# Units of 32 samples throughout a compressed-interaction kernel: triple products as stationary weights in four column groups, 154-column triple-product matmuls, and a GpSimd that only gathers

## The chip, the cores and the metric

The kernel runs on one core of a Trainium2 chip. The metric is device time in microseconds (us). A core has a matrix engine (PE, with its weight loads shown as PEld), a vector engine (DVE), an activation engine (ACT), GpSimd (POOL) and a sync engine that issues DMAs (SP). PE writes to PSUM, here eight banks of 512 fp32 columns by 128 partitions. ACT and DVE copy from PSUM to SBUF. All data is fp32, and in this trace each fp32 matmul leaves two MATMUL records and each pair of them two LDWEIGHTS records; below, a "record" is one of these halves. Transposes leave one.

## What is computed

For 512 samples, 32 embedding rows of 64 numbers are gathered (one from each of 32 tables), and two compressed-interaction layers, each summed over the 64 dimensions, feed a small network of three layers:

```python
# X[b, m, d]: 32 gathered rows of 64 numbers per sample
x1 = einsum('oc,bcd->bod', W0, outer(X, X))   + b0      # 128 outputs
x2 = einsum('oc,bcd->bod', W1, outer(X, x1))  + b1      # 128 outputs
z  = concat([x1.sum(d), x2.sum(d)])                      # (512, 256)
h  = relu([z, dense_ctx] @ W_top1 + b_top1)              # 512
h  = relu(h @ W_top2 + b_top2)                           # 256
y  = h @ W_top3                                          # (512, 1)
```

The kernel doesn't build x1. It uses that x2 summed over d is a sum over triples: T[m, (i, j)] = sum over d of X_m X_i X_j, with a coefficient for each triple and output that is made once from W1 and W0.

## The kernel before

A **unit** is 32 samples, a **chunk** four units; there are 4 chunks, so 16 units, written below as u = 0 to 15 (q = chunk, s = unit in it). All engine programs are written out by hand; the order in each engine's list is the order of execution, and semaphores join them.

**Gathers.** POOL issues 8 indirect DMAs of 128 rows for each unit (L413), into one of four row buffers; it waits only until the buffer's earlier unit has been transposed. At gather 50 (`FOLD_AT`) POOL stops to do two product instructions of unit 3 and six adds of the coefficient fold.

**Per unit.** PE transposes the gathered rows into bank XT (`transpose_rows`, L193, 4 records); this waits for the gathers and until ACT has emptied the bank of the unit before (`xx_ready`, `gram_ready`). ACT copies XT out as `xx` (`act_xx`, L241, two copies) and into the last columns of `prod` (`act_gram`, L250, two copies). DVE multiplies pairs of `xx` into `prod` (`products`, L261 and L265). PE then forms the triple products in four T groups of 8 samples (`t_group`, L212): 32 matmuls each, of 64 rows by 32 weight columns on 77 moving columns, on eight tiles of the array (two row groups, four column groups). Groups 0 and 2 go to one pair of banks, 1 and 3 to the other, so group 2 waits until group 0 has been copied out. ACT copies groups 0 and 2, DVE 1 and 3, each with one instruction of 128 x 616 (`copy_t`, L229 and L226), into `t_sb`.

**Per chunk.** `cin` (L371) multiplies: 77 matmuls with 128 x 128 coefficients as weights and the chunk's 128 samples as moving columns, accumulated in ACC (x2) and ACC + 1 (x1). The chunk before is done in four quarters, one after the T groups of each unit of this chunk. ACT's `copy_z` (L379) adds the bias.

**Phases.** While unit 0 to 3 are worked on, PE also makes the coefficients (L280, L286, 32 pairs of matmuls, copied out by ACT at L292 and DVE at L296). Then these are folded (L306: DVE 18 adds, POOL 6), transposed by PE (L343, 69 matmuls) and copied (L548, L356). From unit 4 on a step is: four T groups, the transposes of unit u + 2, a quarter of `cin`. After unit 15's T groups the last chunk's 77 `cin` matmuls follow, then the network (L474 dense part, L482, L491, L499).

## Time and profile before

| | us |
|---|---|
| median of 3 runs | 257.38 (256.95 to 258.59) |
| the profiled execution's own time | 258.26 |
| its span, first to last instruction | 256.5 |
| mean granted TensorE clock | 0.939 |

| engine | busy us | share of span |
|---|---|---|
| PE | 209.3 | 82% |
| PEld | 173.8 | 68% |
| POOL | 148.8 | 58% |
| DVE | 127.2 | 50% |
| ACT | 84.4 | 33% |

An engine's busy time is the union of its records. A matmul's end is modelled, so for PE the distance between starts of successive records tells more than the length of one. "idle before <-X" names what ended the idle time ahead of an instruction; "issue" means that the profile shows nothing it waited for. The rows themselves stand in a section of their own below.

### The profile page before, as it was taken

What the parts mean: (1) busy time and instruction counts of PE and PEld (TensorE: products, weight loads), DVE (VectorE), ACT (ScalarE), POOL (GpSimd) and SP (SyncE); (2) the same over time, 40 slices, a digit from 0 to 9 for tenths busy, and PEclk for the clock granted to TensorE, in tenths of its full rate; (3) what the DMA queues carried; (4) which work ended last, traced back from release to release, by engine and by line L of the source; (5) the groups of instructions that cost most, each with busy time, mean ns of one, the idle gap of its engine ahead of it and who ended that gap; (6) DMA issues with size and microseconds to landing.
All of it is one profiled execution on the core that took longest, in us unless ns stands there. A gap on an engine that the chain in (4) does not pass through costs nothing.

```text
span 256.5 us, 10809 instructions
## 1 busy us (share of the span) xinstructions
PE 209.3 (82%) x5049; PEld 173.8 (68%) x5049; DVE 127.2 (50%) x194; ACT 84.4 (33%) x159; POOL 148.8 (58%) x142
## 2 busy tenths in 40 slices
PE   7897899499007889799898796979698896999995
PEld 6664667287006769688787584968697796899541
DVE  0559487666920866838649548173918641000000
ACT  2575447264202961413433313142313310100141
POOL 4778788877899778778778778777750000000000
PEclk9999799979856999999999999799889997999999
DMA  6811111112810111111111111111110000000000
GB/s 206 299 26 20 31 28 23 24 33 35 279 22 3 23 26 25 30 23 31 30 24 30 27 24 31 20 32 28 29 26 3 5 3 5 0 3 0 0 0 0
DMA packets 6564, 9.66 MB, mean 38 GB/s; under 512 B 2804, under 2 KB 3256, under 8 KB 6520
## 3 DMA queue, kind: packets, MB, share of 16 engines
q0 software_dynamic: 4096, 4.20, 9.1%
q1 hardware_dynamic: 2136, 4.19, 4.7%
q8 instruction: 39, 0.64, 1.0%
q10 hardware_dynamic: 288, 0.59, 0.7%
q14 instruction: 5, 0.04, 0.0%
HBM read 8.97 MB, written 0.00 MB: 35 GB/s over the span
## 4 chain that ended last, share of the span: by engine, by line
POOL 43%; PE 36%; issue 15%; DMA 3%; ACT 2%; DVE 0%; DVEq 0%; ACTq 0%; POOLq 0%
POOL rows L413 39%; PE psum L371 19%; PE psum L212 7%; PE psum L491 3%; PE psum L482 3%; DMA rows<-table,idx 2%; POOL t_sb L306 2%; POOL prod L261 2%; PE psum L280 1%; PE psum L193 1%; PE psum L286 1%; ACT t_sb L229 1%; DMA t_sb<-ids 1%; PE psum L474 0%; ACT prod L250 0%
## 5 line engine op out<-in xcount | busy, mean ns | idle before, releaser
L413 POOL DMA_INDIRECT rows<-table,idx x128 | 138.8, 1085 | 40.6 <-issue 38.1
L212 PE MATMUL psum<-prod,xx 64*32 64x77 f32 x4096 | 63.7, 243 | 23.7 <-POOL prod L261 13.4
L261 DVE TENSOR_TENSOR prod<-xx 128x1024 f32<-128x1024 f32 x62 | 73.7, 1220 | 6.8 <-ACT xx L241 4.0
L212 PEld LDWEIGHTS psum<-prod,xx 64*32 64x32 f32 x4096 | 51.4, 109 | 35.9 <-issue 16.2
L371 PE MATMUL psum<-t_sb,coef 128*128 128x128 f32 x552 | 67.9, 285 | 2.1 <-issue 2.1
L371 PEld LDWEIGHTS psum<-t_sb,coef 128*128 128x128 f32 x552 | 66.7, 202 | 2.4 <-issue 2.2
L229 ACT ACTIVATE t_sb<-psum 128x616 f32<-128x616 f32 x34 | 23.3, 685 | 79.8 <-PE psum L212 79.8
L226 DVE COPY t_sb<-psum 128x616 f32<-128x616 f32 x30 | 23.9, 798 | 49.8 <-PE psum L212 49.6
L292 ACT ACTIVATE t_sb<-psum 128x276 f32<-128x276 f32 x32 | 20.7, 647 | 18.2 <-PE psum L280 18.0
L241 ACT ACTIVATE xx<-psum 128x512 f32<-128x512 f32 x32 | 17.5, 595 | 24.2 <-PE psum L193 24.2
L280 PE MATMUL psum<-w0p_sb,w_sb 128*128 128x276 f32 x64 | 21.8, 423 | 1.2 <-DVE w0p_sb L592 0.6
L193 PE MATMUL psum<-ident,rows 128*128 128x128 f32 x64 | 10.3, 284 | 13.3 <-DMA rows<-table,idx 9.5
L286 PE MATMUL psum<-w0x_sb,w_sb 128*128 128x256 f32 x64 | 20.5, 402 | 0.7 <-ACT t_sb L292 0.4
L660 DVE COPY prod<-psum 1x128 f32<-1x128 f32 x2 | 0.6, 292 | 41.2 <-PE psum L499 41.2
L296 DVE COPY coef<-psum 128x256 f32<-128x256 f32 x32 | 13.6, 424 | 10.8 <-PE psum L286 10.8
L193 PEld LDWEIGHTS psum<-ident,rows 128*128 128x128 f32 x64 | 6.9, 141 | 16.2 <-DMA rows<-table,idx 11.7
L286 PEld LDWEIGHTS psum<-w0x_sb,w_sb 128*128 128x128 f32 x64 | 10.7, 189 | 7.3 <-ACT t_sb L292 5.1
L280 PEld LDWEIGHTS psum<-w0p_sb,w_sb 128*128 128x128 f32 x64 | 11.4, 196 | 4.3 <-DVE coef L296 1.2
L379 ACT ACTIVATE w_sb<-psum,cin_bias 128x128 f32<-128x128 f32 x8 | 2.9, 368 | 32.3 <-PE psum L371 32.3
L250 ACT ACTIVATE prod<-psum 128x256 f32<-128x256 f32 x32 | 13.1, 408 | 0.0
L343 PE MATMUL psum<-ident,t_sb 128*128 128x128 f32 x69 | 9.2, 289 | 1.5 <-ACT coef L548 1.4
L356 DVE COPY coef<-psum 128x512 f32<-128x512 f32 (+1 forms) x6 | 3.7, 620 | 12.6 <-POOL t_sb L306 11.5
(33 smaller groups left out, 99.9 us busy)
## 6 DMA issues: line engine op xcount, KB each, us to landing
rows<-table,idx POOLq DMA_INDIRECT x128
w_sb<-w1t SPq DMA_DIRECT2D x3, 512.0 KB, 7.0
w_sb<-top SPq DMA_DIRECT2D x2, 512.0 KB, 5.3
t_sb<-w0x ACTq DMA_DIRECT2D x1, 512.0 KB, 4.8
w0x_sb<-w0g SPq DMA_DIRECT2D x1, 512.0 KB, 3.8
w_sb<-w1t SPq DMA_DIRECT2D x1, 384.0 KB, 5.6
t_sb<-w0p SPq DMA_DIRECT2D x1, 276.0 KB, 5.0
w_sb<-w1t SPq DMA_DIRECT2D x1, 128.0 KB, 4.8
```

What stands on the lines that cost most here:

```text
L193: last = pe.matmul(bank(XT, 128 * t, 128), rows[:, c:c + 2 * D], ident[:, :], is_transpose=True, start=True, stop=True)
L212: last = pe.matmul(bank(TG + 2 * (v % 2) + r, n * COLS, COLS, 32 * (2 * e + k), M), xx[s % 2][D * r:D * (r + 1), x:x + M], prod[2 * (s % 2 ...
L226: copy(dst, src).then_inc(t_copied[v % 2], 1)
L229: copy_t(act, lambda o, i: act.activation(o, i, ACT.Copy), q, t_at, s, v)
L241: act.activation(dst, src, ACT.Copy).then_inc(xx_ready, 1)
L261: last = dve.tensor_tensor(at(p, e * COLS, [[2 * COLS, SUB], [HALF, SHIFTS], [1, HALF]]), at(x, x0, [[M, SUB], [0, SHIFTS], [1, HALF]]), a ...
L280: pe.matmul(bank(W_BANKS[2 * x % 3], 0, 4 * VCOLS), w, w0p_sb[:, :], start=True, stop=True)\
L286: pe.matmul(bank(W_BANKS[(2 * x + 1) % 3], 0, HALF * HALF), w, w0x_sb[:, c:c + HALF * HALF], start=True, stop=True).then_inc(u_done, 1)
L292: act.activation(at(t_sb, coef_t_at + x, [[M, 4], [128, VCOLS]]), src, ACT.Copy).then_inc(u_pairs, 1)
L296: dve.tensor_copy(cross[:, x * HALF * HALF:(x + 1) * HALF * HALF], bank(W_BANKS[(2 * x + 1) % 3], 0, HALF * HALF)).then_inc(u_cross, 1)
L371: last = pe.matmul(bank(n, 0, CHUNK), w[:, wc:wc + O], t_sb[:, t_at + tc:t_at + tc + CHUNK], start=first, stop=end)
L413: pool.indirect_dma_start(rows[:, c:c + D], None, table[:, :], bass.IndirectOffsetOnAxis(ap=idx[:, g:g + 1], axis=0))\
```

## The change

Everything is done per unit of 32 samples; chunks are gone.

- **T groups** (`t_group`): the two halves (e) of a sample's pairs stand side by side in `prod` and are now one moving operand of 154 columns. 16 matmuls a group in place of 32. Samples, no longer halves, fill the column groups, so the result lies differently in PSUM.
- **Copies out** (`copy_t`): each group needs four copies of 64 partitions x 308 in place of one of 128 x 616, since partition halves have to change places. ACT does all four of groups 0 and 2 and two of groups 1 and 3; DVE does the other two of groups 1 and 3. For unit 3 ACT does all.
- **`cin_part` and `cin_tile`**: operands swap places. The triple products of 32 samples are the weights (128 rows x 32 columns), the 128 coefficients' outputs move. Matmul i goes to column group i % 4, so that four partial sums stand in four partition groups of one bank. A unit is 77 matmuls in four parts (25, 17, 17, 18), 1,232 in all where `cin` had 308.
- **`copy_acc` and `fold_z`**: DVE copies the four partial sums (128 x 256) to SBUF, and PE multiplies them with four stacked 32 x 32 identities (`fold4`, made by two small DVE adds), which adds them up and turns them round: two matmuls with 128 x 128 weights and 32 moving columns for each unit. ACT's `copy_z` is two copies of 128 x 32 for each unit.
- **Order from unit 4 on**: five `cin` parts a step, two of them between T groups 1 and 2. The transposes of unit u + 2 follow T group 3; for the last four units (`late`) a step transposes unit u + 1 and its `xx`, gram and product work follows in the same step.
- **GpSimd** only gathers. Its two products and six adds go to DVE. The gathers themselves keep their number and size.
- After unit 15's T groups only unit 15's own 77 `cin` matmuls are left before the network.

```diff
-        def t_group(pe, q, s, v):
+        def t_group(pe, u, v):
...
-            wait(pe, t_copied[v % 2], 2 * u + v // 2)
-            for n in range(GROUP // 2):
-                j = (v % 2) * GROUP // 2 + n
-                for k in range(2):
-                    for e in range(2):
+            for n in range(2):
+                wait(pe, t_copied[n], copied(n, 4 * u + v - 1))
+            for n in range(2):
+                for p in range(2):
+                    j = 4 * (v % 2) + 2 * p + n
+                    x, y = (SUB // 2 * g + j) * 2 * M + HALF, 4 * j * COLS
+                    for k in range(2):
                         for r in range(2):
...
+                            last = pe.matmul(bank(TG + 2 * (v % 2) + r, 2 * n * COLS, 2 * COLS, 32 * (2 * p + k), M),
...
+        def copy_t(eng, copy, n, u, v):
+
+            for p in range(2):
+                if copier(4 * u + v, p) != n:
+                    continue
...
+                for e in range(2):
+                    src = at(psum, (TG + 2 * (v % 2)) * BANK + e * COLS, [[1, COLS], [BANK, 2], [2 * COLS, 2]], D * p, D)
+                    dst = at(t_sb, t_at(u) + v * GROUP + 4 * p, [[UNIT, COLS], [2, 2], [1, 2]], D * e, D)
+                    last = copy(dst, src)
+                last.then_inc(t_copied[n], 1)
...
+        def cin_tile(pe, u, j, n, col, w, start, stop):
+            c = t_at(u) + col * UNIT
+            return pe.matmul(at(psum, acc(u) + n * O, [[1, O]], UNIT * j, UNIT), t_sb[:, c:c + UNIT], w,
+                             start=start, stop=stop, tile_position=(0, UNIT * j))
...
+        def copy_acc(eng, copy, u):
+
+            eng.wait_ge(cin_done, u + 1)
+            wait(eng, z_done, u - 1)
+            copy(acc_sb[u % 2][:, :], at(psum, acc(u), [[1, 2 * O]])).then_inc(acc_copied, 1)
+
+        def fold_z(pe, u):
+
+            pe.wait_ge(acc_copied, u + 1)
...
+            for n in range(2):
+                last = pe.matmul(bank(Z, n * UNIT, UNIT), acc_sb[u % 2][:, n * O:(n + 1) * O],
+                                 fold4[:, 0:UNIT], start=True, stop=True)
+            last.then_inc(z_done, 1)
...
+            def parts(start, end):
+                for n in range(start, end):
+                    cin_part(pe, n // 4, n % 4)
+                    if n % 4 == 3 and n > 4:
+                        fold_z(pe, n // 4 - 1)
+
+            for u in range(AHEAD, UNITS):
+                p = PARTS * (u - AHEAD)
+                t_group(pe, u, 0)
+                t_group(pe, u, 1)
+                parts(p, p + 2)
+                t_group(pe, u, 2)
+                t_group(pe, u, 3)
+                if u + 2 < UNITS and not late(u + 2):
+                    transpose_rows(pe, u + 2)
+                if u + 1 < UNITS and late(u + 1):
+                    transpose_rows(pe, u + 1)
+                parts(p + 2, p + PARTS)
...
             for u in range(AHEAD, UNITS):
                 for g in range(2):
                     dve_copy_t(dve, u, 2 * g + 1)
                     if u + 1 < UNITS and not late(u + 1):
                         products(dve, u + 1, g)
                     for x in ended(u, g):
                         copy_acc(dve, dve.tensor_copy, x)
```

PE's list in one step of the second phase, before (L212 is a T group's matmuls, L193 the transposes, L371 `cin`):

```order
L212 MATMUL psum<-prod,xx 32x77 [waits t_copied0,prod_ready,gram_ready]
L212 MATMUL psum<-prod,xx 32x77 x31
L212 MATMUL psum<-prod,xx 32x77 [waits t_copied1]
L212 MATMUL psum<-prod,xx 32x77 x31
L212 MATMUL psum<-prod,xx 32x77 [waits t_copied0,prod_ready,gram_ready]
L212 MATMUL psum<-prod,xx 32x77 x31
L212 MATMUL psum<-prod,xx 32x77 [waits t_copied1]
L212 MATMUL psum<-prod,xx 32x77 x31
L193 MATMUL psum<-ident,rows 128x128 [waits gram_ready,xx_ready,gathered3]
L193 MATMUL psum<-ident,rows 128x128 x3
L371 MATMUL psum<-t_sb,coef 128x128 x19
```

The same engine after the change, unit 6, from its first T group to its transposes and the next `cin` part (L218 T group, L388 `cin_tile`, L404 `fold_z`, L200 transposes):

```order
L218 MATMUL psum<-prod,xx 32x154 [waits t_copied0,t_copied1,prod_ready,gram_ready]
L218 MATMUL psum<-prod,xx 32x154 x15
L218 MATMUL psum<-prod,xx 32x154 [waits t_copied1,t_copied0]
L218 MATMUL psum<-prod,xx 32x154 x15
L388 MATMUL psum<-coef,t_sb 32x128 x35
L404 MATMUL psum<-fold,acc_sb 128x32 [waits z_copied,acc_copied]
L404 MATMUL psum<-fold,acc_sb 128x32
L218 MATMUL psum<-prod,xx 32x154 [waits t_copied0,t_copied1,prod_ready,gram_ready]
L218 MATMUL psum<-prod,xx 32x154 x15
L218 MATMUL psum<-prod,xx 32x154 [waits t_copied1,t_copied0]
L218 MATMUL psum<-prod,xx 32x154 x15
L200 MATMUL psum<-ident,rows 128x128 [waits gram_ready,xx_ready,gathered0]
```

Two `cin` parts, and in this unit a fold, now stand between T groups 1 and 2. The transposes wait for the same semaphores at the same place, after T group 3.

ACT's list in one step of the second phase, before (L229 is `copy_t`, L250 `act_gram`, L241 `act_xx`):

```order
L229 ACTIVATE t_sb<-psum 128x77x2x4 [waits t_done]
L250 ACTIVATE prod<-psum 128x32x8 [waits t_done,xt_done]
L229 ACTIVATE t_sb<-psum 128x77x2x4 [waits t_done]
L250 ACTIVATE prod<-psum 128x32x8 [waits t_done,xt_done]
L241 ACTIVATE xx<-psum 128x512 [waits t_done,xt_done] x2
```

ACT after the change, the second half of a step, which is groups 2 and 3 and what follows (L244 `copy_t`, L263 `act_gram`, L411 `copy_z`, L255 `act_xx`):

```order
L244 ACTIVATE t_sb<-psum 64x77x4 [waits t_done,coef_tr]
L244 ACTIVATE t_sb<-psum 64x77x4
L244 ACTIVATE t_sb<-psum 64x77x4 [waits t_done,coef_tr]
L244 ACTIVATE t_sb<-psum 64x77x4
L244 ACTIVATE t_sb<-psum 64x77x4 [waits t_done,coef_tr]
L244 ACTIVATE t_sb<-psum 64x77x4
L263 ACTIVATE prod<-psum 128x32x8 [waits t_done,xt_done]
L411 ACTIVATE w_sb<-psum,cin_bias 128x32 [waits z_done]
L411 ACTIVATE w_sb<-psum,cin_bias 128x32
L255 ACTIVATE xx<-psum 128x512 [waits t_done,xt_done] x2
```

Six copies, the last two of them of group 3, stand ahead of the gram copy where one stood.

DVE after the change, unit 6 (L240 `copy_t`, L273 and L277 `products`, L395 `copy_acc`):

```order
L240 COPY t_sb<-psum 64x77x4 [waits t_done,coef_tr]
L240 COPY t_sb<-psum 64x77x4
L273 TENSOR_TENSOR prod<-xx 128x16x64 [waits t_done,xx_ready]
L273 TENSOR_TENSOR prod<-xx 128x16x64
L277 TENSOR_TENSOR prod<-xx 128x32x4
L395 COPY acc_sb<-psum 128x256 [waits cin_done]
L240 COPY t_sb<-psum 64x77x4 [waits t_done,coef_tr]
L240 COPY t_sb<-psum 64x77x4
```

The copy of the partial sums stands behind the products of the next unit's first half.

## Rows read from the trace of the kernel before

**Rows 1.** The page: engines' busy time, share of the span, instructions.
```profile
PE 209.3 (82%) x5049; PEld 173.8 (68%) x5049; DVE 127.2 (50%) x194; ACT 84.4 (33%) x159; POOL 148.8 (58%) x142
```
**Rows 2.** Waits, whole span: who waited for whom, us, times, longest.
```profile
POOL rows L413 <- issue: 38.1, 125, 0.3
...
PE psum L212 <- POOL prod L261: 13.4, 1, 13.4
...
PE psum L212 <- issue: 8.2, 8, 1.3
```
**Rows 3.** POOL's gathers by line, then POOL in the timeline: start, us, engine.
```profile
L413 POOL DMA_INDIRECT rows<-table,idx x128: 940/945/1976, 3.5 to 189.3; - x128
...
73.94 3.98 POOL L261 TENSOR_TENSOR prod<-xx 128x1024 f32<-128x1024 f32 x2
...
77.89 5.39 POOL L306 TENSOR_TENSOR t_sb<-t_sb,coef 128x512 f32<-128x512 f32 x6
```
**Rows 4.** Timeline: a unit's last gather, the transposes that wait for it.
```profile
156.43 1.32 POOL L413 DMA_INDIRECT rows<-table,idx  x1 [0.30 <-issue]
...
157.41 0.69 PE L212 MATMUL psum<-prod,xx 64*32 64x77 f32 x39 [1.08 <-issue]
...
159.32 0.66 PE L193 MATMUL psum<-ident,rows 128*128 128x128 f32 x4 [1.23 <-DMA rows<-table,idx]
```
**Rows 5.** Timeline: end of the first phase, start of the second.
```profile
62.78 7.94 DVE L306 TENSOR_TENSOR t_sb<-t_sb,coef 128x1024 f32<-128x1024 f32 x18
...
83.36 0.60 ACT L548 ACTIVATE coef<-psum 128x512 f32<-128x512 f32 x1 [2.29 <-POOL t_sb L306]
...
91.37 3.16 PE L212 MATMUL psum<-prod,xx 64*32 64x77 f32 x192
```
**Rows 6.** Timeline: the step of unit 14, and the start of unit 15's.
```profile
199.21 1.57 PE L212 MATMUL psum<-prod,xx 64*32 64x77 f32 x128
...
200.15 0.68 ACT L229 ACTIVATE t_sb<-psum 128x616 f32<-128x616 f32 x1 [3.99 <-PE psum L212]
...
200.73 0.40 ACT L250 ACTIVATE prod<-psum 128x256 f32<-128x256 f32 x1
...
203.75 4.51 PE L371 MATMUL psum<-t_sb,coef 128*128 128x128 f32 x38
...
208.19 1.57 PE L212 MATMUL psum<-prod,xx 64*32 64x77 f32 x128
```
**Rows 7.** Groups by line and shape: count | busy us, mean ns | idle before.
```profile
L261 DVE TENSOR_TENSOR prod<-xx 128x1024 f32<-128x1024 f32 x62 | 73.7, 1220 | 6.8 <-ACT xx L241 4.0 <-issue 2.8
...
L212 PE MATMUL psum<-prod,xx 64*32 64x77 f32 x4096 | 63.7, 243 | 23.7 <-POOL prod L261 13.4 <-issue 8.2 <-ACT t_sb L229 1.0
L212 PEld LDWEIGHTS psum<-prod,xx 64*32 64x32 f32 x4096 | 51.4, 109 | 35.9 <-issue 16.2 <-POOL prod L261 13.6 <-DVE t_sb L226 1.3
L226 DVE COPY t_sb<-psum 128x616 f32<-128x616 f32 x30 | 23.9, 798 | 49.8 <-PE psum L212 49.6
L229 ACT ACTIVATE t_sb<-psum 128x616 f32<-128x616 f32 x34 | 23.3, 685 | 79.8 <-PE psum L212 79.8
...
L241 ACT ACTIVATE xx<-psum 128x512 f32<-128x512 f32 x32 | 17.5, 595 | 24.2 <-PE psum L193 24.2
L296 DVE COPY coef<-psum 128x256 f32<-128x256 f32 x32 | 13.6, 424 | 10.8 <-PE psum L286 10.8
L250 ACT ACTIVATE prod<-psum 128x256 f32<-128x256 f32 x32 | 13.1, 408 | 0.0
```
**Rows 8.** Timeline: the last layer, four column groups, 128 rows, 128 moving columns.
```profile
252.49 0.40 PE L499 MATMUL psum<-prod,top_sb 128*1 128x128 f32 x8
```
**Rows 9.** Timeline: the last chunk's `cin` and the network's first layer.
```profile
223.25 15.57 PE L371 MATMUL psum<-t_sb,coef 128*128 128x128 f32 x138
...
238.66 7.03 PE L482 MATMUL psum<-w_sb 128*128 128x512 f32 x16
```
**Rows 10.** One stretch: busy of PE, PEld, DVE, ACT, POOL, granted clock, DMA, GB/s.
```profile
152.90:165.80 12.90, 10.57 (x303) 9.51 (x302) 6.54 (x8) 3.04 (x6) 10.16 (x10) 0.87 0.14 28
```

More of the change, by code:

```diff
@@ L364, in cin, with cin_part @@
+        def cin_part(pe, u, part):
             if part == 0:
-                for p in range(2):
-                    pe.wait_ge(t_copied[p], (c + 1) * UNITS * 2)
-                wait(pe, acc_free, 2 * c)
+                for n in range(2):
+                    pe.wait_ge(t_copied[n], copied(n, 4 * (u + 1)))
+                wait(pe, acc_copied, u - 1)
                 for n in range(2):
                     pe.wait_ge(coef_ready[n], COPIER.count(n))
-            for n, w, wc, tc, first, end in CIN[len(CIN) * part // 4:len(CIN) * (part + 1) // 4]:
-                last = pe.matmul(bank(n, 0, CHUNK), w[:, wc:wc + O], t_sb[:, t_at + tc:t_at + tc + CHUNK],
-                                 start=first, stop=end)
-                if end:
-                    last.then_inc(cin1_done if n == ACC + 1 else t_free, 1)
@@ L376, in copy_z @@
[L376 to L386 removed]
+                for i in range(GRAM):
+                    cin_tile(pe, u, i % 4, 0, PAIRS + i, w0g_sb[:, i * O:(i + 1) * O], i < 4, i >= GRAM - 4)
@@ new lines, in copy_z, with ended @@
+        def copy_z(act, u):
+            act.wait_ge(z_done, u + 1)
+            for n in range(2):
+                last = act.activation(at(w1_sb, z_at + n * B + u * UNIT, [[1, UNIT]]),
+                                      bank(Z, n * UNIT, UNIT),
+                                      ACT.Identity, bias=cin_bias[:, 2 + n:3 + n])
+            last.then_inc(z_copied, 1)
+        def ended(u, g):
+            n = PARTS * (u - AHEAD)
+            return [x for x in range(UNITS - 1) if (n <= 4 * x + 3 < n + 2 if g else n - PARTS + 2 <= 4 * x + 3 < n)]
@@ L388, in _, with late @@
+        def late(u):
+            return u >= UNITS - 4
         @block.gpsimd
@@ L471, in _ @@
-            pe.wait_ge(gram_ready, 2 * CHUNKS * UNITS)
-            pe.wait_ge(t_copied[0], CHUNKS * UNITS * 2)
-            for j in range(TOP1 // 128):
-                pe.matmul(bank(L1 + j), w1_sb[32 * j:32 * j + DENSE, top1d_at:top1d_at + 128],
-                          w1_sb[32 * j:32 * j + DENSE, dense_at:dense_at + B], start=True, stop=False)
-            for part in range(4):
-                cin(pe, c, c % 2 * COLS * CHUNK, part)
+            def parts(start, end):
[3 more added lines that the diff above has]
+                        fold_z(pe, n // 4 - 1)
@@ L646, in step @@
-            def step(q, s, ahead, t_at):
-                for g in range(2):
-                    dve_copy_t(dve, q, t_at, s, 2 * g + 1)
-                    if ahead[1]:
-                        products(dve, *ahead[1], g)
+            dve.wait_ge(ident_ready, 1)
+            dve.tensor_tensor(at(fold4, UNIT, [[UNIT, 2], [1, UNIT]]), at(ident, 0, [[UNIT, 2], [1, UNIT]]),
+                              at(ident, 2 * UNIT, [[UNIT, 2], [1, UNIT]]), ALU.add).then_inc(fold4_step, 1)
+            dve.wait_ge(fold4_step, 1)
@@ L653, in _ @@
+            dve.tensor_tensor(fold4[:, 0:UNIT], fold4[:, UNIT:2 * UNIT], fold4[:, 2 * UNIT:3 * UNIT], ALU.add)\
+                .then_inc(fold4_ready, 1)
             dve.wait_ge(small_in_sb, 32)
             dve.tensor_scalar(cin_bias[:, 2:4], cin_bias[:, 0:2], float(D), None, ALU.mult).then_inc(bias_ready, 1)
-            for c in range(1, CHUNKS):
-                chunk(lambda q, s, ahead: step(q, s, ahead, q % 2 * COLS * CHUNK), c, final=c == CHUNKS - 1)
+            for u in range(AHEAD, UNITS):
+                for g in range(2):
+                    dve_copy_t(dve, u, 2 * g + 1)
+                    if u + 1 < UNITS and not late(u + 1):
+                        products(dve, u + 1, g)
+                    for x in ended(u, g):
+                        copy_acc(dve, dve.tensor_copy, x)
+                if u + 1 < UNITS and late(u + 1):
+                    for g in range(2):
+                        products(dve, u + 1, g)
```

305 lines of the change are left out of this document (148 added, 157 removed).

## The prediction

> **What bounds the kernel now.** I read the engines' busy times first: PE is busy 82% of the span, POOL 58%, ACT only 33% [rows 1]. A busy PE is not yet the bound, so next the waits and the gathers. POOL's 128 gathers run from 3.5 to 189.3 us with a pause of 0.3 us ahead of each and no wait for a free buffer [rows 2, 3]. POOL's own products and adds interrupt them for 3.98 + 5.39 = 9.4 us [rows 3]; the rest, (185.8 - 9.2) / 127, is 1.39 us a gather, 11.1 us a unit. The last gather of a unit starts at 156.43 and the transposes that wait for it run at 159.32, so rows land about 2.8 us after that start [rows 4]. Until the last unit the gathers and PE run about level: a step of PE without a wait takes 9.0 us (199.21 to 208.19) [rows 6]. After the gathers there are still T groups, and after unit 15's T groups (start 208.19) 48.3 us of PE alone, of which the last chunk's coefficients take 15.57 and more, and the network 17.8 (238.66 to 256.46) [rows 6, 9]. One wait stands out: PE stood 13.4 us for two product instructions that POOL reached late [rows 2]. So there are three things to gain: POOL's 9.4 us, PE's 13.4 us, and the tail.
>
> **T groups.** 4,096 records take 63.7 us, 15.5 ns each; with a filled queue 128 of them start within 1.57 - 0.23 us, 10.6 ns each [rows 6, 7]. The stream itself is shorter: 16 records of 512 columns in 7.03 us are (7.03 - 0.59) / 15 = 0.43 us each, 0.84 ns a column [rows 9]; 77 columns on eight tiles are 8.1 ns a record. So instructions bound it, not columns. With 154 columns a record costs 16.2 ns of stream on eight tiles, and a group has 32 records: 0.53 us in place of 0.67 to 1.0. PE is busy some 29 us less over 64 groups. In this kernel's steps much of that was wait for copies, so I go by steps below.
>
> **`cin`.** Before, 38 records in 4.51 us are 0.114 us apart [rows 6], 616 of them 70 us. After, 2,464 records on four column groups. The nearest row is the last layer: the same 128 rows, four column groups, 128 moving fp32 columns, and its 8 records last 0.40 us with 0.27 for one, so they start within 0.13 us [rows 8]; one after the other they would need 7 x 0.114 = 0.80. Hence four records per 0.114 us, 28.5 ns each, 70 us again: 1.1 us for a part, 4.4 for a unit. Its weights have one column, here 32; the T groups' 32-column loads show that width loading beside running matmuls [rows 7]. Bounds: 28.5 ns, and 114 if nothing overlapped.
>
> **New work.** `fold_z` is four records with 128-column weights and 32 moving columns, priced like the transposes' four (0.66 us, [rows 4]), so 0.6 us with the changes of shape around it, 1.25 times a step. ACT's copies: its 512 and 256 wide ones take 595 and 408 ns [rows 7], 0.73 ns a column on 221 fixed, so 308 columns take 0.45; successive ACT copies start 0.10 us before the end of the one before (200.15 + 0.68 against 200.73 [rows 6]), so 0.35 each. Twelve a step are 4.2 us where two took 1.2. No row shows 64 partitions with runs of two samples; the bounds are 0.30 (half of the 616 wide one) and 0.58 (no gain for half the width). DVE's two copies a group take 0.9 us, about what its one took; `copy_acc` is 424 ns [rows 7].
>
> **First phase.** Units 0 to 2 stay bound by gathers. DVE's fold started at 62.78 [rows 5]; DVE now has two products of 1.22 us [rows 7] more ahead of it, partly in its idle time, and I add 1.5 us. Its 18 adds took 7.94 us [rows 5]; POOL's six, at DVE's rates, add 2.6: 64.3 + 10.5 = 74.8. From the first coefficient copy to the first T group of unit 4 it took 83.36 to 91.37, 8.0 us [rows 5], with the same work. Unit 4 starts at 82.8, not 91.4.
>
> **A step from there**, times from its start. Groups 0 and 1 end at 1.05. Two `cin` parts to 3.3. ACT starts to copy at 0.86 (0.94 before, of which the group was 0.67 [rows 6]), has group 0 at 2.4, its half of group 1 at 3.1: group 2 starts without wait at 3.4, group 3 ends at 4.45. ACT begins group 2 at 4.26, ends groups 2 and 3 at 6.5 and the gram copy at 6.8. The transposes wait for just that copy. Here a wait appears that hardly existed: PE stands from 4.45 to 6.8. Queued behind it are three `cin` parts, which need nothing. Then transposes to 7.4, three parts to 10.6, folds: 11.3 us. In units 6 and 10 the fold stands between groups 1 and 2 and its `copy_acc` behind DVE's products, done at 5.2 where PE comes at 3.3: 2 us more. Late steps transpose unit u + 1, whose bank is long empty: no gram wait, but ACT (7.0), then 2.65 us of products give 9.7. Sums: units 4 to 9 10.7 + 11.3 + 13.3 + 11.9 + 11.3 + 11.3 = 69.8; unit 10 (no transposes) 10.5; 11 to 14 10.3 + 9.7 + 9.7 + 10.3 = 40.0. Unit 15 starts at 82.8 + 69.8 + 10.5 + 40.0 = 203.1. Gathers are not in the way: unit 15's land at 3.5 + 127 x 1.39 + 2.8 = 182.9.
>
> **Tail.** Unit 15's step 8.9, `cin` 4.4 and a fold 0.6, three dense matmuls 0.8, `copy_acc` and the last fold 1.0, `copy_z` 0.6, fourth dense 0.2: first layer at 219.6, plus 17.8 is 237.4 before the clock.
>
> **Clock.** PE waits of 1.08 and 1.23 us two us apart [rows 4] stood in a step of 12.9 us with a mean granted clock of 0.87 [rows 10], where the step of rows 6 took 9.0. Six steps now wait 2.4 us. I take three falls to 1.2 GHz at 1.7 us: 5 us. Span 242.4, against 256.5: 14.1 less. The median of the runs shown is 257.4, 0.9 above the profiled span, so 243.
>
> **Rivals.**
> *The gram wait doesn't cost what I say* (ACT copies near 0.30, the clock stays up, folds hidden). Then the gathers bound the end: unit 15 lands at 182.9, T groups 4.2 us later (transposes, xx, products), plus 34.3 for step and tail: 221 to 232. For it: POOL never waited. Against: the order of ACT's list. 0.14.
> *ACT binds* at 0.58 a copy: groups 2 and 3 take 1.4 us more ahead of the gram copy or the late `xx`; over 11 steps 15 us: 258. Against: half the columns never cost the full copy in any row. 0.08.
> *Column groups don't load beside each other* (the slower side). All four tiles of `cin` use the same 128 rows; if a tile's weights could only load when no matmul runs on these rows, four records would take 0.114 + 0.109 (the mean 32-column load [rows 7]), 56 ns each, +67 us: 309. It decides from 35 ns a record on, where 2,464 x 6 ns eat the 14 us. Against: the 128-column weights of `cin` already load during the matmul before on the same rows, or 38 records couldn't stand 0.114 apart. 0.07.
> The Trainium skill speaks for this rival: "TensorE: Matmul & The Clock Gate", Part 3, says that a weight load overlaps a running matmul only where the row group differs. By that rule the time is this rival's 309. This trace disagrees at full width.
> *The merge does nothing*, instructions staying the bound: 154 columns need 16.2 ns of stream anyway, so at most 1 us a step.
>
> **Numbers.** My case 0.71, alone 233 to 252; the gathers' 0.14, ACT's 0.08, the loads' 0.07. The range cuts the last and half of ACT's and a part of the first: 229 to 256. A measurement of this kernel tells about 1% from no change. Faster: 0.71 + 0.14 + a little of ACT's, less the edge of mine, 0.85; same 0.06; slower 0.09.
>
> **What the new profile would show.** T records of 154 columns 16 ns apart; L388 28 to 29 ns apart, 70 us in all; L244 0.45 us; PE at L200 waiting for the gram copy L263, some 2.4 us in six steps; unit 4 at 83, unit 15 at 203; L440 done near 181 without a gap; DVE's folds 10.5 us. Wrong if L388 stands over 35 ns apart, if L244 takes 0.6, or if PE waits for gathers from unit 8 on.

## The result, and the profile after

| | before | after |
|---|---|---|
| median, 4 runs each (us) | 257.76 (256.95 to 258.59) | 268.48 (267.83 to 270.44) |
| profiled span | 256.5 | 267.1 |
| mean granted clock | 0.939 | 0.911 |

The changed kernel is slower: ratio 1.043, 95% interval 1.036 to 1.050. I had predicted 243, with 256 as the upper end. Ratios below are taken over those runs of a kernel that lie within 1.5% of its fastest, so they aren't always the quotient of the medians; where too few such runs were left, none is given.

The page of after: busy time by engine, PE's granted clock in 40 slices (tenths), the chain that ended last, and groups that carry the sum (count | busy us, mean ns | idle before).

```profile
PE 218.9 (82%) x4913; PEld 169.7 (64%) x4913; DVE 145.9 (55%) x248; ACT 147.9 (55%) x345; POOL 137.6 (52%) x134
...
PEclk9999799979759979986979797979979999999799
...
PE 56%; ACT 12%; issue 11%; POOL 9%; DVE 8%; DMA 2%; DVEq 0%; ACTq 0%
...
L244 ACT ACTIVATE t_sb<-psum 64x308 f32<-64x308 f32 x196 | 82.4, 420 | 66.9 <-PE psum L218 64.3
...
L388 PE MATMUL psum<-coef,t_sb 128*32 128x128 f32 x2208 | 77.0, 288 | 0.6 <-issue 0.5
...
L218 PE MATMUL psum<-prod,xx 64*32 64x154 f32 x2048 | 46.0, 307 | 8.0 <-issue 5.0 <-ACT t_sb L244 2.8
```

PE has 136 fewer records than before [rows 1] and is busy for 9.6 us more: its T groups fell from 63.7 us [rows 7] to 46.0, but all of `cin` together went from 76.3 to 85.4, and the folds are 10.1 us of new work. Stretches at the low clock are part of these times. In the clock line a 7 comes at every second slice in the middle (slices 21, 23, 25 and 27). The rates that I had feared are near the forecast: ACT's copy is 420 ns, and where the clock is full `cin`'s records follow each other at 27.5 ns within a run, 30.1 with what lies between runs. What changed is in the waits (who waited for whom: us, times, longest):

```profile
PE psum L200 <- ACT prod L263: 16.7, 6, 2.9
...
PE psum L218 <- issue: 5.0, 4, 1.9
...
PE psum L404 <- DVE acc_sb L395: 4.2, 2, 2.1
```

The second line is PE's wait ahead of the T groups of units 12 to 15, which start right after DVE's products (193.81 after a product that ends at 193.71). The wait of the transposes for ACT's gram copy, forecast at 14.1 us in six steps, is there with 16.7. Unit 5's step in the timeline (start, us), rows of the step that matter:

```profile
99.08 1.29 PE L218 MATMUL psum<-prod,xx 64*32 64x154 f32 x64
...
100.00 2.61 ACT L244 ACTIVATE t_sb<-psum 64x308 f32<-64x308 f32 x6 [5.02 <-PE psum L218]
...
100.30 2.16 PE L388 MATMUL psum<-coef,t_sb 128*32 128x128 f32 x68
...
102.38 1.31 PE L218 MATMUL psum<-prod,xx 64*32 64x154 f32 x64
...
103.45 2.60 ACT L244 ACTIVATE t_sb<-psum 64x308 f32<-64x308 f32 x6 [0.40 <-PE psum L218]
...
106.08 0.40 ACT L263 ACTIVATE prod<-psum 128x256 f32<-128x256 f32 x1
...
106.63 0.63 PE L200 MATMUL psum<-ident,rows 128*128 128x128 f32 x4 [2.93 <-ACT prod L263]
107.19 1.29 PE L388 MATMUL psum<-coef,t_sb 128*32 128x128 f32 x36
```

PE is done with the T groups by 103.7, the second gram copy runs at 106.08, behind ACT's twelve copies. The three `cin` parts that stand behind the transposes, from 107.19 on, had their data all that time. This step took 12.4 us at full clock. Others didn't stay there. Stretches of after (busy of PE, PEld, DVE, ACT, POOL, then granted clock): all of phase 2 up to unit 15's T groups, unit 5's step, unit 6's, unit 7's, unit 8's, and the network:

```profile
85.30:228.20 142.90, 116.20 (x3617) 99.76 (x3617) 81.12 (x127) 80.06 (x201) 72.56 (x71) 0.90 0.10 20
...
99.08:111.49 12.41, 9.48 (x326) 8.21 (x325) 7.51 (x11) 6.95 (x16) 9.67 (x10) 1.00 0.16 31
...
111.49:127.40 15.91, 11.20 (x327) 9.43 (x325) 7.96 (x12) 7.62 (x20) 12.24 (x13) 0.79 0.15 28
...
127.40:141.70 14.30, 11.49 (x338) 9.75 (x336) 7.47 (x11) 7.28 (x18) 11.27 (x10) 0.88 0.12 25
...
141.70:155.90 14.20, 11.45 (x341) 9.79 (x340) 7.47 (x11) 7.27 (x18) 10.85 (x12) 0.88 0.14 27
...
247.52:267.10 19.58, 16.43 (x49) 6.81 (x48) 0.58 (x2) 4.66 (x8) 0.00 (x0) 0.91 0.00 0
```

If all of the missing clock is lost time, phase 2 lost 0.10 x 142.9 = 14 us and the network 0.09 x 19.6 = 1.8. That is an upper bound: PE was at 1.2 GHz for 27.3 us of phase 2, but stood idle for 4.0 of them, so by its busy time there the loss is 11.6 us. The steps bear the size out: those of units 5 and 8 were forecast alike and differ by 1.8 us, with 1.00 and 0.88. Before, the same stretch of phase 2 (91.37 to 208.19) had 0.97, 3.5 us:

```profile
91.37:208.19 116.82, 99.69 (x3279) 89.69 (x3279) 71.80 (x92) 35.01 (x71) 76.95 (x73) 0.97 0.13 24
```

I keep the kernels that the argument needs in three sums, in us. They add up to the profiled span.

| kernel | unit 4 starts | unit 4 to unit 15 | unit 15's start to the end | span |
|---|---|---|---|---|
| before | 91.4 | 116.8 | 48.3 | 256.5 |
| predicted (clock's 5 us shared out nowhere) | 82.8 | 120.3 | 34.3 | 242.4 |
| after | 85.3 | 142.9 | 38.9 | 267.1 |
| gram_early | 83.9 | 121.1 | 38.9 | 243.9 |
| pe_order | 83.1 | 122.8 | 38.6 | 244.5 |
| filler | 84.5 | 135.1 | 36.6 | 256.2 |
| split77 | 85.3 | 162.0 | 42.6 | 289.9 |
| before_pool_only | 84.9 | 115.0 | 46.4 | 246.3 |

After itself was not run again beside the experiments. The kernel before took 257.8 to 260.5 us on their three chips and 257.76 beside after, so comparisons of an experiment with after carry about 1%.

The two things that were to gain did gain: 6.1 us at unit 4's start and 9.4 behind unit 15's. The middle lost 26.1. So the question for the experiments is the middle.

### The profile page after: what moved, and what is told of

Its sections match the earlier page's. It is cut to its first block, busy times and chain, and to the rows that moved or that the text cites. A ratio compares the mean times of both kernels' runs of the same rounds, so it can differ in the third digit from the quotient of the medians.

```text
span 267.1 us, 10973 instructions
## 1 busy us (share of the span) xinstructions
PE 218.9 (82%) x4913; PEld 169.7 (64%) x4913; DVE 145.9 (55%) x248; ACT 147.9 (55%) x345; POOL 137.6 (52%) x134
## 3 DMA queue, kind: packets, MB, share of 16 engines
q0 software_dynamic: 4096, 4.20, 8.0%
## 4 chain that ended last, share of the span: by engine, by line
PE 56%; ACT 12%; issue 11%; POOL 9%; DVE 8%; DMA 2%; DVEq 0%; ACTq 0%
PE psum L388 26%; PE psum L218 13%; POOL rows L440 9%; ACT t_sb L244 7%; DVE t_sb L318 4%; PE psum L527 3%; PE psum L404 3%; PE psum L200 3%; PE psum L352 3%; DVE prod L273 3%; PE psum L536 3%; ACT prod L263 2%; DMA rows<-table,idx 1%; PE psum L298 1%; ACT t_sb L304 1%
## 5 line engine op out<-in xcount | busy, mean ns | idle before, releaser
L244 ACT ACTIVATE t_sb<-psum 64x308 f32<-64x308 f32 x196 | 82.4, 420 | 66.9 <-PE psum L218 64.3
L273 DVE TENSOR_TENSOR prod<-xx 128x1024 f32<-128x1024 f32 x64 | 76.4, 1223 | 11.0 <-ACT xx L255 10.6
L388 PE MATMUL psum<-coef,t_sb 128*32 128x128 f32 x2208 | 77.0, 288 | 0.6 <-issue 0.5
L388 PEld LDWEIGHTS psum<-coef,t_sb 128*32 128x32 f32 x2208 | 68.0, 117 | 6.2 <-issue 5.3
L240 DVE COPY t_sb<-psum 64x308 f32<-64x308 f32 x60 | 28.8, 480 | 58.0 <-PE psum L218 57.3
L218 PE MATMUL psum<-prod,xx 64*32 64x154 f32 x2048 | 46.0, 307 | 8.0 <-issue 5.0
L218 PEld LDWEIGHTS psum<-prod,xx 64*32 64x32 f32 x2048 | 33.2, 109 | 16.9 <-issue 14.7
L200 PE MATMUL psum<-ident,rows 128*128 128x128 f32 x64 | 12.4, 327 | 19.0 <-ACT prod L263 16.7
L304 ACT ACTIVATE t_sb<-psum 128x276 f32<-128x276 f32 x32 | 20.1, 649 | 9.8 <-PE psum L292 9.3
L255 ACT ACTIVATE xx<-psum 128x512 f32<-128x512 f32 x32 | 17.9, 597 | 11.0 <-PE psum L200 10.9
L200 PEld LDWEIGHTS psum<-ident,rows 128*128 128x128 f32 x64 | 8.5, 164 | 22.8 <-issue 19.5
L298 PEld LDWEIGHTS psum<-w0x_sb,w_sb 128*128 128x128 f32 x64 | 10.9, 195 | 14.0 <-ACT t_sb L304 12.6
L352 PE MATMUL psum<-ident,t_sb 128*128 128x128 f32 x69 | 12.0, 353 | 3.5 <-DVE t_sb L318 2.5
L404 PE MATMUL psum<-fold,acc_sb 128*128 128x32 f32 x64 | 10.1, 281 | 5.0 <-DVE acc_sb L395 4.2
L404 PEld LDWEIGHTS psum<-fold,acc_sb 128*128 128x128 f32 x64 | 8.3, 190 | 9.0 <-DVE acc_sb L395 6.5
L352 PEld LDWEIGHTS psum<-ident,t_sb 128*128 128x128 f32 x69 | 11.1, 187 | 4.4 <-issue 2.8
L263 ACT ACTIVATE prod<-psum 128x256 f32<-128x256 f32 x32 | 13.3, 417 | 0.4
```

The lines of the kernel that those rows point to most:

```text
L200: last = pe.matmul(bank(XT, 128 * t, 128), rows[:, c:c + 2 * D], ident[:, :], is_transpose=True, start=True, stop=True)
L218: last = pe.matmul(bank(TG + 2 * (v % 2) + r, 2 * n * COLS, 2 * COLS, 32 * (2 * p + k), M), xx[u % 2][D * r:D * (r + 1), x:x + M], prod[2 ...
L240: last = copy(dst, src)
L244: copy_t(act, lambda o, i: act.activation(o, i, ACT.Copy), 0, u, v)
L273: last = dve.tensor_tensor(at(p, e * COLS, [[2 * COLS, SUB], [HALF, SHIFTS], [1, HALF]]), at(x, x0, [[M, SUB], [0, SHIFTS], [1, HALF]]), a ...
L298: pe.matmul(bank(W_BANKS[(2 * x + 1) % 3], 0, HALF * HALF), w, w0x_sb[:, c:c + HALF * HALF], start=True, stop=True).then_inc(u_done, 1)
```

## The experiments

My theory after reading the trace: the wait for the gram copy costs the middle twice, once by its own length, once by the clock that falls after it. Rivals: the steps are long because of their many small instructions (then the wait's removal gains little), and the clock falls because of what PE runs (T groups, changes of array shape), not because of its waits.

### Both gram copies early on ACT

```diff
...
-                    if u + 1 < UNITS and not late(u + 1):
-                        act_gram(act, u + 1, g)
+                    if g == 0 and u + 1 < UNITS and not late(u + 1):
+                        act_gram(act, u + 1, 0)
+                        act_gram(act, u + 1, 1)
```

> ACT makes both gram copies of the next unit right after the copies of T group 1, nothing else moves. Theory A (PE's wait for the gram copy behind ACT's six T copies, 16.7 us in six waits, and the clock falls that follow these waits are what the change costs): the six waits go, and with them most of the six falls to 1.2 GHz of 3.4 us each, worth up to 1.7 us each: 268.5 - 16.7 - 5 to 10 = 242 to 247 us, granted clock 0.94 or more. Rival B (ACT is the bound; the wait only moves to the T groups, which wait for copies): above 262 us. Rival C (the clock falls because PE does less in each us, not because of these waits): the waits go, the clock stays at 0.91: about 252 us.

Measured: 244.98 us (243.27 to 247.03), ratio to before 0.940 (0.929 to 0.951). The wait of the transposes for ACT is gone from the list, and phase 2 takes 121.1 us in place of 142.9, its clock is 0.96. Theory A's 242 to 247 held; rival B wanted more than 262 and rival C a clock of 0.91. One ACT instruction of 0.4 us a step, moved ahead of six others in its list, is worth 23 us of span. That is the whole loss of the change and more.

### The same wait removed from the other side, on PE

ACT's list is left as it was. PE's transposes of unit u + 2 go behind all five `cin` parts:

```diff
-                if u + 2 < UNITS and not late(u + 2):
-                    transpose_rows(pe, u + 2)
                 if u + 1 < UNITS and late(u + 1):
                     transpose_rows(pe, u + 1)
-                parts(p + 2, p + PARTS)
+                parts(p + 2, p + 5)
+                if u + 2 < UNITS and not late(u + 2):
+                    transpose_rows(pe, u + 2)
+                parts(p + 5, p + PARTS)
```

> PE's list alone is changed: in units 4 to 9 the transposes of unit u + 2 stand behind all five cin parts of the step instead of behind two. The gram copy on ACT keeps its late place. Theory (the wait of 2.8 us is a matter of order, and the clock falls after it): three cin parts of 1.1 us fill the wait, PE L200 waits for ACT L263 under 3 us in all in place of 16.7, half-clock stretches in units 4 to 9 shrink to one or two, and the time comes down near that of the kernel with the early gram copies (244.98): 243 to 250, though xx and products of unit u + 2 come 3 us later, which nothing needs soon. Rival 1 (PE has the same work to do in either order and the T groups of the next step inherit the wait, since ACT is late anyway): over 262. Rival 2 (the clock falls for another reason than the wait, T groups' many small matmuls): the wait goes but the half-clock time stays above 40 us, 255 to 262.

Measured: 246.29 us (242.0 to 249.94, 4 runs), the kernel before on the same chip 260.16 (253.85 to 261.53, 7 runs). No ratio with an interval came out of these runs, but the two ranges don't touch, and the time is in the 243 to 250 that the theory gave. Rivals 1 and 2 both fell: the first wanted over 262, the second 255 to 262 and a slow clock. The timeline of unit 7's step in this kernel, all of PE and the gram copy:

```profile
126.27 1.41 PE L218 MATMUL psum<-prod,xx 64*32 64x154 f32 x64
...
127.61 0.64 PE L388 MATMUL psum<-w0x_sb,t_sb 128*32 128x128 f32 x16
...
128.07 2.13 PE L388 MATMUL psum<-coef,t_sb 128*32 128x128 f32 x68
...
130.14 1.37 PE L218 MATMUL psum<-prod,xx 64*32 64x154 f32 x64
...
131.44 2.17 PE L388 MATMUL psum<-coef,t_sb 128*32 128x128 f32 x70
...
133.53 0.63 PE L404 MATMUL psum<-fold,acc_sb 128*128 128x32 f32 x4
133.72 0.41 ACT L263 ACTIVATE prod<-psum 128x256 f32<-128x256 f32 x1
...
135.81 0.66 PE L200 MATMUL psum<-ident,rows 128*128 128x128 f32 x4
```

The gram copy is as late as ever (133.72, against 131.5 for the last T record), but PE has 4.4 us of `cin` and fold to do meanwhile. No row of PE has a wait. The step and the phase, with the clock before the last two columns:

```profile
83.10:205.90 122.80, 110.30 (x3617) 94.52 (x3617) 80.97 (x126) 79.52 (x201) 77.52 (x73) 0.97 0.12 23
126.30:136.40 10.10, 10.10 (x343) 8.74 (x342) 7.47 (x11) 7.17 (x18) 7.91 (x8) 1.00 0.15 31
```

The same step took 14.3 us in after. The two steps below 1.0 that are left are those of units 6 and 10 (0.87 and 0.86). Unit 6's holds this wait for `copy_acc`:

```profile
107.63 0.63 PE L404 MATMUL psum<-fold,acc_sb 128*128 128x32 f32 x4 [2.19 <-DVE acc_sb L395]
```

### The wait kept, but filled

To part the wait from the clock, PE got 12 matmuls (24 records) ahead of the transposes of units 6 to 11, which stand in for the idle time:

```diff
...
+                    for n in range(12):
+                        pe.matmul(at(psum, acc(x) + (O if open_ else 2 * O), [[1, O]]), zero[:, :], coef[:, 0:O],
+                                  start=not open_, stop=not open_)
                     transpose_rows(pe, u + 2)
```

> Before the transposes of units 6 to 11 PE does 12 matmuls of 128 x 128 zero weights on 128 columns (2.6 us at full clock), which add nothing to the result, inside the wait for the gram copy. Theory A's second half (the waits make the clock fall): the waits stay filled, the clock stays up in these six steps, and the time falls by 6 x 1.7 = 10 us at most, to 258 to 262 us, granted clock 0.94 or more. Rival C (the clock falls for another reason): 268 us or more, clock 0.91, or worse, since filler at half clock runs past the wait.

Measured: 257.71 us (255.15 to 263.34, 10 runs), just under the 258 to 262 expected; ratio to before 0.990 (0.984 to 0.996). The clock over the whole kernel is 0.952 to 0.987 in these ten runs; in the four of after it was 0.911 to 0.927. Unit 7's step in the timeline, and the whole of phase 2 as a stretch:

```profile
140.56 1.47 PE L220 MATMUL psum<-prod,xx 64*32 64x154 f32 x64
141.96 2.95 PE L508 MATMUL psum<-coef,zero 128*128 128x128 f32 x24
144.74 0.60 PE L202 MATMUL psum<-ident,rows 128*128 128x128 f32 x4
```

```profile
84.50:219.60 135.10, 124.23 (x3767) 108.88 (x3771) 81.15 (x127) 80.09 (x201) 76.94 (x72) 0.99 0.10 21
```

The fillers last as long as the wait did, so the steps still hold it; yet the clock is 0.99 in the phase in place of 0.90, and the span is 10.9 us shorter than after's. Seventeen us of useless matrix work made the kernel faster. Not all of the 10.9 us can be put down to them: 0.8 lies before the first filler, and 2.3 behind unit 15's start, 1.7 of it in the first layer, which ran as fast in share_copies below without any filler. From 256.2 to pe_order's 244.5 are another 11.7 us: the wait itself. In phase 2 alone the fillers gave 7.8 us and the wait's removal another 12.3, so of the 20.1 us between after and pe_order there the clock is somewhat under half. The fillers cost something too: unit 5's step, at 1.00 in both kernels, took 12.8 us with them and 12.4 without. With 0.4 us in six steps added, the clock's part of phase 2 is 10 us by this experiment, 11.6 by PE's busy time at 1.2 GHz, 14 by the missing clock; I can't say more closely.

### Fewer copies on ACT

DVE takes two of the four copies of groups 0 and 2 as well, so ACT has eight a step in place of twelve.

```diff
-            return int(p == 1 and group % 2 == 1 and group // 4 != AHEAD - 1)
+            return int(p == 1 and (group % 2 == 1 or group // 4 >= AHEAD) and group // 4 != AHEAD - 1)
...
             for u in range(AHEAD, UNITS):
                 for g in range(2):
+                    dve_copy_t(dve, u, 2 * g)
                     dve_copy_t(dve, u, 2 * g + 1)
```

> From unit 4 on DVE also takes two of the four copies of T groups 0 and 2, so that ACT has four copies ahead of the gram copy and of the late xx in place of six: 0.87 us less at 0.43 each. Theory A: eleven steps are 0.87 us shorter and a few clock falls go with it: 255 to 260 us. Rival D (DVE, now with four copies of 0.48 us ahead of its products, becomes the wait): 266 us or more, with PE waiting for products.

Measured: 257.49 us (254.66 to 264.71, 4 runs; before on that chip 260.52). The wait is shorter and not gone, 11.6 us in the six steps with a longest of 1.9:

```profile
PE psum L200 <- ACT prod L263: 11.6, 6, 1.9
```

ACT's four copies last 1.73 us there, its six 2.60 in after: 0.43 us each, one after the other. The time is in the 255 to 260 of theory A, and rival D (266 or more) fell. Phase 2 takes 134.2 us in place of 142.9, 5.1 of it shorter gram waits, and its clock is 0.92. So less of ACT's work helps; the place of one copy in the list counts for more.

### The merged T groups taken back

Each 154-column matmul of the T groups is again two of 77 columns, with nothing else changed.

```diff
-                            last = pe.matmul(bank(TG + 2 * (v % 2) + r, 2 * n * COLS, 2 * COLS, 32 * (2 * p + k), M),
...
+                            for e in range(2):
+                                last = pe.matmul(bank(TG + 2 * (v % 2) + r, (2 * n + e) * COLS, COLS, 32 * (2 * p + k), M),
...
```

> The T groups again as 32 matmuls of 77 columns, everything else as changed. If instructions bound a T group, as read in the trace before (10.6 to 15.5 ns a record against 8.1 of stream), each pair of groups takes 1.5 to 2.0 us in place of 1.2, and a step loses 0.6 to 1.5 us where the groups are on the path: 276 to 284 us. Rival (merging saves nothing, since 154 columns stream as long as two times 77 are issued): 268 us.

Measured: 291.91 us (289.29 to 296.31), ratio 1.121 (1.106 to 1.135). The merge is worth some 23 us in this kernel against this way of splitting it, more than the 8 to 16 that I expected:

```profile
L219 PE MATMUL psum<-prod,xx 64*32 64x77 f32 x4096 | 73.9, 235 | 11.2 <-issue 10.0 <-ACT t_sb L245 1.0
```

The 4,096 records are 73.9 us of busy time. After has 46.0 for its 2,048, the kernel before had 63.7 for as many as here [rows 7]; the records of a pair of groups, which start within 1.0 us merged, took 1.8 to 4.0 here with the waits among them. PE's waits ahead of T records with no named releaser are 10.0 us in 12 places, where after has 5.0 in 4 and the kernel before had 8.2 in 8 [rows 2]. Why these records stand less densely than those of the kernel before, I didn't settle: the order of the two halves differs too.

### Before, with a GpSimd that only gathers

The one part of the change that stands alone: POOL's two products and six adds go to DVE, in the kernel before.

```diff
-        DVE_SHIFTS, POOL_SHIFTS = range(0, 6), range(6, 8)
+        DVE_SHIFTS = range(0, 8)
...
-                        products(pool, 0, 3, 1, 0)
-                        products(pool, 0, 3, 1, 1).then_inc(pool_prod, 1)
-                        pool.wait_ge(u_pairs, M)
-                        pool.wait_ge(u_cross, M)
-                        fold_first(pool, POOL_SHIFTS, pool_step)
-                        pool.wait_ge(pool_step, 1)
-                        fold_second(pool, POOL_SHIFTS, pool_step)
...
```

> The kernel before with one part of the change: GpSimd only gathers, DVE does the two products of unit 3 and the adds of shifts 6 and 7. Theory: the gathers end 9.4 us earlier, the first phase ends 6 to 7 us earlier, and since the steps of before are partly bound by gathers and partly by PE, the whole is 6 to 9 us faster: ratio 0.965 to 0.975. Rival (DVE's longer fold eats it, or PE bounds the steps alone): ratio above 0.985.

Measured: 249.81 us (248.13 to 253.1), ratio 0.971 (0.960 to 0.982), inside the 0.965 to 0.975 expected. Unit 4 starts at 84.9, as in the changed kernel. So this part gives some 8 us, and the other parts of the change as it was made cost some 19 on top of it.

### Towards the best order

Three more edits on gram_early, one after the other. First no late steps, so that all transposes run two units ahead:

```diff
-            return u >= UNITS - 4
+            return u >= UNITS
```

> gram_early, and the last four units' transposes come two steps ahead like the others'. Theory: in late steps PE waits because xx, gram and products of the next unit start only when ACT has done the six T copies; with the work a step ahead, units 11 to 14 take 9.6 to 10 us a step in place of 10.5 to 12.4, until the gathers bind: unit 15's rows land near 183, its T groups start at 196 to 198, 7 to 9 us before gram_early: 236 to 238 us. Rival (the late order is there because gathers are late; PE then waits as long for gathers): 243 us or more, with DMA waits ahead of the transposes.

Measured: 243.85 us (241.69 to 245.0), ratio 0.947 (0.939 to 0.956); in the profiled executions unit 15 starts at 200.6 in place of 205.0, and the span is 239.9 in place of 243.9. PE's wait ahead of the late T groups is 0.5 us in place of 4.9. But the ratio is no better than gram_early's (0.940), so the gain isn't shown, and the time is far from the 236 to 238 expected: PE waits 4.0 us for gathers, 2.1 before. Then also DVE's `copy_acc` ahead of its products, against the 2 us wait of the folds:

```diff
-                    if u + 1 < UNITS and not late(u + 1):
-                        products(dve, u + 1, g)
                     for x in ended(u, g):
                         copy_acc(dve, dve.tensor_copy, x)
+                    if u + 1 < UNITS and not late(u + 1):
+                        products(dve, u + 1, g)
```

> gram_nolate, and DVE copies the partial sums before it does the products, so that the fold between T groups 1 and 2 of units 6 and 10 doesn't wait 2.1 us. Theory: units 6 and 10 are 2.5 us shorter each and one or two clock falls go; if the gathers bind from unit 12 on, only a part of it is left at the end: 2 to 5 us faster than gram_nolate, 232 to 236 us. Rival (gathers bind already): no change from gram_nolate.

Measured: 240.03 us (239.58 to 242.01), ratio 0.935 (0.927 to 0.944): 3.8 us less than without this edit, as expected, though not the 232 to 236 that I had put down. Unit 6's step went from 13.0 to 10.6 us. The limit is another one now. The page's chain by engine, and a wait:

```profile
POOL 58%; PE 20%; issue 17%; DMA 2%; ACT 1%; POOLq 1%; DVE 0%; DVEq 0%; ACTq 0%
```

```profile
PE psum L200 <- DMA rows<-table,idx: 6.9, 4, 2.2
```

The chain that ended last is mostly POOL's gathers. With DVE sharing ACT's copies on top of all that (the diff of share_copies):

> gram_nolate_acc, and DVE shares the copies of all four T groups with ACT. Theory: with the gram copy early ACT is no longer ahead of anything that PE waits for, so sharing brings at most 1 us: 231 to 236 us. Rival (group 2's start or ACT's xx is still bound by ACT's copies): 4 us or more faster than gram_nolate_acc.

Measured: 242.5 us (239.64 to 245.87), ratio 0.939 (0.929 to 0.949), the same as without, and not the 231 to 236 expected. With the gram copy early, sharing ACT's copies gains nothing. Last, the transposes behind two more `cin` parts, to give the gathers time:

```diff
-                parts(p + 2, p + PARTS)
+                parts(p + 2, p + 4)
+                if u + 2 < UNITS and not late(u + 2):
+                    transpose_rows(pe, u + 2)
+                parts(p + 4, p + PARTS)
```

> Early gram copies, no late steps and copy_acc ahead of the products, as in the kernel measured at 240.03, and the transposes of unit u + 2 moved behind two more cin parts. There PE waited 6.9 us in four stretches for gathers ahead of the transposes, from unit 9 on. Theory A (with this order the gathers land in time, since each transpose stands 2.2 us later in its step): the DMA waits fall to 1 to 4 us, unit 15's T groups start 2 to 4 us earlier, at 195 to 197, and the span is 233 to 236, the time 234 to 238. Theory B (gathers bind: unit 15's rows land at 184 whatever stands ahead; transposes, xx and products of unit 15 then give its T groups after one more step): unit 15 starts at 198 as before, the time is within 1% of 240.

Measured: 240.23 us (237.12 to 244.01), ratio 0.931 (0.902 to 0.959). On the time theory B held, within 1% of 240. Unit 15 starts at 203.6 in this profile, and at 200.2 in that of best2_tail below, which has the same order up to there; gram_nolate_acc had 198.6. PE still waits for gathers, 7.9 us in five places, and POOL's share of the chain is 59%:

```profile
PE psum L200 <- DMA rows<-table,idx: 7.9, 5, 3.4
```

In best2_tail's profile these waits are 3.6 us in two places, and unit 15 is no earlier than in gram_nolate_acc for it. Moving work about in PE's list doesn't help where the rows land when they land. And eight matmuls around the last fold that only keep PE busy:

```diff
...
+            fill(4)
             fold_z(pe, last_u)
+            fill(4)
```

> best2 with eight matmuls of 128 x 128 on a bank that is free by then, four on either side of the last fold, whose result nobody reads (extra work, nothing left out). Theory A (the clock fell in the first layer because PE stood for copy_acc, fold and copy_z just ahead of it, 0.5 to 1.5 us each): the first layer L527 runs in 7.0 to 7.2 us in place of 8.8 to 10.2, no half-clock stretch after unit 15's cin, and the whole is 1.5 to 3 us faster than best2. Theory B (the fall comes from what stands further ahead, or the extra matmuls delay what PE would do in these waits): L527 stays at 8.8 or more, or the time is the same or up to 1 us longer.

Measured: 241.65 us (239.64 to 243.74), ratio 0.948 (0.930 to 0.967). The first layer is as short as theory A said, the time is not: it wanted 1.5 to 3 us less than best2. The first row is best2's first layer, the second that of the kernel with the fillers:

```profile
222.60 8.83 PE L528 MATMUL psum<-w_sb 128*128 128x512 f32 x16
```

```profile
219.93 7.13 PE L534 MATMUL psum<-w_sb 128*128 128x512 f32 x16
```

The 1.7 us are less than the runs of these two kernels differ among themselves, so on the time nothing is shown. Nor is it shown that these matmuls made the layer short: it also took 7.13 us in filler and share_copies, which have nothing added there, and 8.77 to 10.15 in the other kernels with the new tail.

## Why the prediction was wrong, point by point

**What held.** The T groups: the records of a pair start within 1.0 us at full clock, and the next work starts 1.22 us after the first (1.05 forecast). Over the whole kernel that took 17.7 us off PE's busy time, not the 29 of the text. `cin` with four column groups: 138 of the last unit's 154 records stand from 239.50 to 244.22 with a fold of 0.56 between, 30.1 ns each with the changes to what follows, 27.5 within a run ((2.17 - 0.27) / 69), 28.5 forecast. So the rival of 309 us, loads that wait for each other, is refuted, and with it what that sentence of the Trainium skill ("TensorE: Matmul & The Clock Gate", Part 3) would give for this case: loads onto the same 128 rows did run beside matmuls on those rows. These are the rows of the last unit:

```profile
239.50 2.14 PE L388 MATMUL psum<-coef,t_sb 128*32 128x128 f32 x68
241.56 0.63 PE L404 MATMUL psum<-fold,acc_sb 128*128 128x32 f32 x4
242.12 2.17 PE L388 MATMUL psum<-coef,t_sb 128*32 128x128 f32 x70
244.22 1.13 PE L456 MATMUL psum<-w_sb 16*128 16x512 f32 x6
```

POOL's gathers ended early (last start 178.2), DVE's fold took about the 10.5 us forecast (22 of its 24 adds from 65.49 to 75.78), and the two new waits stand in the very places that the text named: six gram waits, two fold waits.

**The step that failed: "I take three falls to 1.2 GHz at 1.7 us: 5 us."** By the missing clock phase 2 and network lost 14 + 1.8 = 16 us (12 with the fillers' figure for phase 2), so this term was 7 to 11 us short. Three falls at 1.7 us are 10.2 us at 1.2 GHz; phase 2 had 27.3, in the steps of seven units (4, 6 with the longest, 7, 8, 9, 10 and 12). The reasoning was inconsistent: [rows 10] had shown a step at 0.87 with waits of 1.08 and 1.23 us, I forecast six of 2.35, and then took half of them to have no effect. By the row's own example, each of the six steps and the two fold waits should have had its fall, 8 x 1.7 = 14 us, and the network's one more. The comparison with rows 6 also misread them: that step is not one without a wait, PE stands idle in it for 0.20 and 1.00 us, and it has no transposes. The filler experiment shows that the falls follow the idle time and not the work around it. Not each wait had one: unit 5's step, with 2.93 us idle, ran at 1.00, and unit 6's, with two waits, at 0.79.

**ACT's copies were mis-sized: "so 0.35 each".** A copy lasts 0.42 us (0.45 forecast), but the overlap that the 616-wide one showed isn't there: six in 2.61 us. The gram copy thus ended at 7.4 us of the step, not at 6.8, and the wait was 2.8, not 2.35. The 0.43 lies between the 0.35 of my sum and the 0.58 of ACT's rival.

**The steps' remainder.** Phase 2 took 22.6 us more than the 120.3 of the steps. With 14 of it for the clock, the eleven steps took some 9 us more than forecast (13 by the fillers' figure): 2.6 of it the longer gram waits, the rest 0.6 us a step on the average. It is not spread evenly: units 11 to 14 took 46.2 us, forecast 40.0, and one stretch at low clock explains 1.7 of that at most; the rest, 4.5 us, is half of the remainder, in the late steps, where PE waited 5.0 us for products. In unit 5's step the remainder shows in pairs of 1.22 us in place of 1.05 and the three parts and fold from 107.19 to 111.49, 4.3 us in place of 3.9. The rates within a run of like records are as forecast, and the trace of this step shows where the time goes: 0.22 us between the starts of the last T record and the first of `cin`, 0.20 from `cin` back to the T groups, where within a run no distance is over 0.12. So I put this down to the changes from one shape to the next; no experiment tested the cause.

**Unit 4's start** was 2.5 us late (85.3, forecast 82.8): DVE's fold began at 65.5 where I had 64.3, and what follows it took 9.5 us, not 8.0, at a clock of 0.72, where the 8.0 us of before had 1.00. In the other kernels it is 83.1 to 85.3. **The tail** from unit 15's start 38.9, forecast 34.3: 2.8 in `cin`, folds and changes of shape, the rest the clock in the first layer.

The sum, with the missing clock as the measure: 11 (clock) + 9 (steps) + 2.5 (unit 4) + 2.8 (tail) = 25, and the span missed by 24.7. With the fillers' figure the clock is 7 and the steps 13. Either way both terms failed; which was the larger stays open. gram_early, which has no gram wait, speaks for some 10 us of steps: its phase 2 of 121.1 us less 5 for the clock is 116, where the forecast less its 14.1 us of waits is 106.2. That its span of 243.9 is so near the predicted 242.4 is luck: it lacks the waits that the sum held, and holds about as much that the sum left out.

**What the chances should have been.** The forecast that PE stands from 4.45 to 6.8 in six steps, with three `cin` parts queued behind that need nothing, was right, and I priced little but its length. No rival let all of these waits cost the clock. This was the mechanism on the other side of zero, at 242.4 - 5 + 16 = 253 with the terms else as forecast, and over 256 with 0.3 us more a step. The range ended there.

## What to carry to other kernels

Before pricing a wait, look at what is queued behind it on its engine: where that work has its data, the wait is a matter of order, and one moved line (0.4 us of ACT, or four transposes of PE) was worth 22 to 23 us here. Where PE is the bound and runs near its top clock, count each new idle stretch of two or three us twice, by its length and by the clock that the next rows are granted; a trace that shows one fall after a 1.2 us wait has told you so. And a change of four parts should be timed in parts: the same change with one copy moved is 6% faster than before, as it was made 4% slower.

## What the runs showed of the hardware

- Idle time of PE lowers its clock, and useless matmuls in the idle time keep it up: 0.90 to 0.99 over phase 2, which got 7.8 us shorter with 17.7 us of added matmuls in it. Not every wait was followed by a fall: unit 5's of 2.93 us wasn't.
- A 32-column weight load with 128 rows hides behind matmuls on three other column groups of the same rows: the last unit's records at 27.5 ns each within a run, 30.1 with what lies between runs.
- ACT's copies of 64 x 308 from PSUM follow each other at 0.43 us with 0.42 for one, where the 128 x 616 one of before let its successor start 0.10 us before its end [rows 6].
- The same columns in half as many records took PE 46.0 us of busy time in place of 73.9, and the whole 23 us less. The kernel before needed 63.7 for as many records as the split one, in another order.
